# Expert-weight loads on ScalarE's queue in the last attention unit, rebalanced one-hots and a later rank sum, in a cross-attention and expert-mixture kernel

## What is computed

```python
def _L0_xattn_ref(q, k, v):            # 8 rows of one sequence are one head
    qh = q.reshape(b * h, d // h, m); kh = k.reshape(b * h, d // h, -1); vh = v.reshape(b * h, c // h, -1)
    qk = jnp.einsum('bdm,bdn->bmn', qh, kh) * scale
    sm = jax.nn.softmax(qk, axis=-1)
    return jnp.einsum('bmn,bcn->bcm', sm, vh).reshape(b, c, m)

def _L0_ffn_ref(x, gate_kernel, w0_kernel, w1_kernel, wo_kernel):   # 8 experts, top 2
    top_k_weights, top_k_indices = jax.lax.top_k(jnp.einsum('bsd,de->bse', x, gate_kernel), 2)
    top_k_weights = jax.nn.softmax(top_k_weights, axis=-1)
    combine = jnp.einsum('bsk,bske->bse', top_k_weights, jax.nn.one_hot(top_k_indices, 8))
    inter = jax.nn.silu(einsum(x, w0_kernel)) * einsum(x, w1_kernel)
    return jnp.einsum('bse,bsem,emd->bsd', combine, inter, wo_kernel)

x = x + _L0_xattn_ref(_layernorm(x), ctx_2048, ctx_2048)
x = x + _L0_ffn_ref(_layernorm(x), gate, w0, w1, wo)
```

## Time and profile before

| | us |
|---|---|
| median of 3 runs | 489.21 |
| lowest, highest | 484.64, 489.81 |
| the profiled execution | 489.81 |
| its span in the trace | 488.1 |

### The profile page before, as it was taken

One profiled execution on the slowest core, in us unless ns is written; L12 is line 12 of the kernel. 1 busy time (PEld: TensorE's weight loads), 2 busy tenths in 40 slices (PEclk: granted clock), 3 DMA queues, 4 the chain that ended last, 5 costly groups with the idle time before them and its releaser, 6 DMA issues.

```text
span 488.1 us, 10784 instructions
## 1 busy us (share of the span) xinstructions
PE 426.1 (87%) x3468; PEld 212.4 (44%) x3469; DVE 303.1 (62%) x636; ACT 267.1 (55%) x529; POOL 219.9 (45%) x244
## 2 busy tenths in 40 slices
PE   4857999889899999998666799999999999999991
PEld 4322343324343444333232455555555555566650
DVE  7799898898888888976867734343434343222220
ACT  2555898778778788977414444444444444222220
POOL 9544322181809052339628233454545454536231
PEclk9775899989889999999867999999999999999997
DMA  8757569685859682426994112333333333323322
GB/s 246 215 165 201 153 165 215 205 245 173 247 165 245 178 255 75 151 71 234 395 389 150 36 34 45 42 57 43 54 47 50 49 50 53 55 45 46 41 22 23
DMA packets 42246, 65.03 MB, mean 133 GB/s; under 512 B 6297, under 2 KB 32218, under 8 KB 42202
## 3 DMA queue, kind: packets, MB, share of 16 engines
q1 hardware_dynamic: 28570, 38.49, 28.0%
q0 software_dynamic: 11328, 23.86, 20.9%
q10 hardware_dynamic: 2304, 2.10, 1.4%
HBM read 39.53 MB, written 24.58 MB: 131 GB/s over the span
## 4 chain that ended last, share of the span: by engine, by line
PE 67%; DVE 10%; ACT 7%; DMA 6%; POOL 4%; issue 2%; ACTq 1%; SPq 1%; DVEq 0%; POOLq 0%
PE max_ps L1658 19%; PE pv_ps L1525 9%; PE pv_ps L1680 6%; PE ring_ps L1508 6%; ACT pt L851 5%; PE max_ps L1652 4%; PE max_ps L1384 4%; PE ring_ps L1680 4%; DVE mx L1026 4%; PE ring_ps L1616 3%; PE ring_ps L1405 2%; PE ring_ps L1675 2%; DMA Q<-mrow 2%; DMA Q<-q_img 2%; PE ring_ps L1416 2%
## 5 line engine op out<-in xcount | busy, mean ns | idle before, releaser
L1026 DVE TENSOR_REDUCE mx<-max_ps 128x4 f32<-128x1024 f32 x128 | 150.7, 1218 | 20.7 <-PE max_ps L1384 20.6
L851 ACT ACTIVATE pt<-ring_ps 128x512 f32<-128x512 f32 x256 | 139.2, 599 | 32.6 <-PE ring_ps L1508 29.1
L1658 PE MATMUL max_ps<-w_sb,pt 128*128 x224 | 101.6, 596 | 1.0 <-issue 1.0
L778 POOL DMA_INDIRECT out<-rb,sidx x34 | 54.8, 1613 | 81.3 <-DVE rb L1358 37.0
L1525 PE MATMUL pv_ps<-pt,w_sb 128*27 128x256 f32 (+2 forms) x1024 | 82.7, 408 | 0.7 <-ACT pvs L861 0.4
L1330 DVE TENSOR_TENSOR pt<-pt,max_ps 128x512 f32<-128x512 f32 x34 | 23.4, 688 | 68.4 <-issue 49.2
L1384 PE MATMUL max_ps<-K,Q 48*128 48x256 bf16 x512 | 54.5, 294 | 12.2 <-DVE mx L1026 12.0
L1508 PE MATMUL ring_ps<-Q,K 50*128 50x256 f16 x512 | 53.4, 289 | 11.5 <-ACT pt L851 9.2
L1658 PEld LDWEIGHTS max_ps<-w_sb,pt 128*128 128x128 f32 x224 | 40.3, 190 | 42.2 <-issue 42.0
L935 ACT ACTIVATE pt<-ring_ps 128x512 f32<-128x512 f32 x34 | 20.3, 598 | 68.1 <-PE ring_ps L1616 68.1
L1508 PEld LDWEIGHTS ring_ps<-Q,K 50*128 50x128 bf16 x512 | 15.1, 96 | 65.3 <-ACT pt L851 58.2
(11 more groups left out here) (230 smaller groups left out, 650.6 us busy)
## 6 DMA issues: line engine op xcount, KB each, us to landing
w_sb<-in_L_ffn_w_kernel POOLq DMA_DIRECT2D x16, 512.0 KB, 12.4
K<-k_img SPq DMA_DIRECT2D x14, 448.0 KB, 6.2
Q<-q_img SPq DMA_DIRECT2D x14, 448.0 KB, 7.6
k_img<-kpart SPq DMA_DIRECT2D x28, 192.0 KB, 3.8
q_img<-qpart SPq DMA_DIRECT2D x28, 192.0 KB, 3.4
wo_sb<-in_L_ffn_wo_kernel POOLq DMA_DIRECT2D x8, 512.0 KB, 14.4
acc<-pvs SPq DMA_DIRECT2D x6, 512.0 KB, 3.1
wo_sb<-in_ctx ACTq DMA_DIRECT2D x16, 128.0 KB, 3.9
```

The lines of the kernel that those rows point to most:

```text
L778: g.indirect_dma_start(xacc, bass.IndirectOffsetOnAxis(ap=sidx[sl.par][:, 0:1], axis=0), y_sb[sl.par], None, compute_op=ALU.add).then_inc( ...
L851: a.activation(pt[:, (2 * i + h) % PTN, :, :], bank(key)[:, :, :], ACT.Exp, scale=SCALE).then_inc(ring_read, 1)
L1026: v.tensor_reduce(mx[:, t % 2, :, :, p].rearrange("q mt h -> q h mt"), max_ps[n % 2][:, :, :, :], axis=AX.X, op=ALU.max).then_inc(max_read, 1)
L1658: last = nc.tensor.matmul(flat(max_ps[sl.par][:, bank_of]), lhsT=xT[sl.par][:, k * P:(k + 1) * P], rhs=weight(w, e, KC, k), start=(k == 0) ...
```

## The change

1. The 24 weight loads go from GpSimd to ScalarE. In tile 15 they stand behind each pair's exponentials and copies: w0(p) and wo(p) in each pair p, and w1(p - 2) too from pair 2. w1 of experts 6 and 7 come behind the last copy of the attention's output. GpSimd keeps the three powers.
2. In tile 15 the transposes and logits of units ST-3 and ST-2 stand one pair later, `unpermute(2)` one pair earlier, rank 0 in pair 6 (from pair 2). Rank 1 goes from pair 7 behind the transposes and logits of tile 14, with two wide matmuls into pv_ps behind it. VectorE's sum of rank 0 moves behind the norm of tile 14, that of rank 1 behind the norm of tile 15.
3. The one-hots are shared 17 (VectorE), 9 (ScalarE) and 6 (GpSimd), before 16, 8 and 8.
4. The spares are turned on TensorE ahead of the first transposes of slot 0 and reduced by VectorE ahead of the four products of line 1271. They are spread in slot 0 (TensorE) and read there by VectorE. Before this was in slots 0 and 1.

```diff
-    rows_at[T - 1, 1] = ST - 3
-    logits_at[T - 1, 2] = ST - 3
-    rows_at[T - 1, 3] = ST - 2
-    logits_at[T - 1, 4] = ST - 2
-    unperm_at = {(T - 2, 1): 0, (T - 2, 4): 1, (T - 1, 2): 2}
+    rows_at[T - 1, 2] = ST - 3
+    logits_at[T - 1, 3] = ST - 3
+    rows_at[T - 1, 4] = ST - 2
+    logits_at[T - 1, 5] = ST - 2
+    unperm_at = {(T - 2, 1): 0, (T - 2, 4): 1, (T - 1, 1): 2}
-    ranks_at = {(T - 1, 2): 0, (T - 1, 7): 1}
+    ranks_at = {(T - 1, 6): 0}
...
-        by_act = [(k, t) for k in range(TOPK) for t in range(2, T, 4)]
-        by_pool = [(k, t) for k in range(TOPK) for t in range(3, T, 4)]
+        by_act = [(0, t) for t in (3, 7, 11, 14)] + [(1, t) for t in (2, 5, 8, 11, 14)]
+        by_pool = [(0, t) for t in (5, 10, 15)] + [(1, t) for t in (4, 9, 13)]
+        by_dve = [(k, t) for k in range(TOPK) for t in range(T) if (k, t) not in by_act + by_pool]
...
@@ gpsimd @@
-            rows_landed(T - 1)
-            load_each(load_w0, range(E))
             rsqrt_last(0, 2, 1)
-            load_each(load_wo, range(4, E))
-            load_each(load_w1, range(3))
             rsqrt_last(2, 3, 2)
-            load_each(load_w1, range(3, E - 1))
-            load_each(load_wo, range(2))
             rsqrt_last(3, 4, 3)
-            load_w1(E - 1)
-            load_each(load_wo, range(2, 4))
...
@@ scalar, end of each pair's pass @@
+                if t == T - 1:
+                    if p == 0:
+                        a.wait_ge(mrow_in[1], T // 2 * 32)
+                    load_w0(p)
+                    load_wo(p)
+                    if p >= 2:
+                        load_w1(p - 2)
             evac_pv(T - 1)
+            load_w1(E - 2)
+            load_w1(E - 1)
...
@@ vector @@
             norm_last(normed_last[0:2], x2_last[0:2], 0, 1)
-            ranks(0)
...
             norm_last(normed_last[2:3], x2_last[2:3], 2, 2)
-            ranks(1)
+            ranks(0)
...
             norm_last(normed_last[3:4], x2_last[3:4], 3, 3)
+            ranks(1)
             choose(ST, unit_tiles[ST])
...
+            v.wait_ge(spare_turned, 1)
+            then(v.tensor_reduce(spare_any[:, :], y_ps[1][0:NT, 0, P // 2:P].bitcast(f16), axis=AX.X, op=ALU.max))
+            v.tensor_tensor(spare_diag[:, :], identh[0:NT, 0:NT], spare_any[:, 0:1].broadcast_to([NT, NT]),
+                            ALU.mult).then_inc(diag_done, 1)
             v.wait_ge(rows_picked, TOPK)
...
@@ tensor @@
             for m in range(ST - 1, UNITS):
                 turn_rows(m)
                 logits(m)
+                if m < UNITS - 1:
+                    rank(1)
+                    keep_warm(2, pv_ps)
...
             pe.wait_ge(slots_done, 1)
+            turn_spares()
             turn_x(Slots(0, 0))
...
                 if sl.peeled and sl.t == 0:
-                    turn_spares()
+                    spread_spares()
                 if sl.peeled and sl.t == 1:
-                    spread_spares()
                     slot_weights()
```

More of the change, by code:

```diff
@@ L649, in rsqrt @@
                 g.tensor_tensor(rstd[:, a:b], veps[:, a:b], mhalf[:, a:b], ALU.pow).then_inc(rstd_done, 1)
[L651 to L673, removed]
             g.wait_ge(consts, 2)
@@ L809, in _, with load_w0, load_w1, load_wo @@
         def _(a):
+            def load_w0(e):
+                a.dma_start(w0_sb[:, KC * e:KC * e + KC, :], w0_view[:, KC * e:KC * e + KC, :]).then_inc(w_in, 16)
+            def load_w1(e):
+                a.wait_ge(pv_full, 8 * (2 * e + 2))
+                a.dma_start(w1_sb[:, KC * e:KC * e + KC, :], w1_view[:, KC * e:KC * e + KC, :]).then_inc(w_in, 16)
+            def load_wo(e):
+                if e < E // 2:
+                    a.wait_ge(k_split, ST)
+                    for m in range(ST):
+                        a.wait_ge(ring_read, slots["v", m] + 1)
+                a.dma_start(wo_sb[:, FC * e:FC * e + FC, :], wo_view[:, FC * e:FC * e + FC, :]).then_inc(w_in, 16)
+            def load_each(load, experts):
+                for e in experts:
+                    load(e)
             def evac_v(g):
@@ L1232, in _ @@
                                 iota_t[:, None, :].broadcast_to([P, T, NTL]), ALU.is_equal).then_inc(rows_picked, 1)
-                onehots(k, [t for t in range(T) if (k, t) not in by_act and (k, t) not in by_pool])
+                onehots(k, [t for n, t in by_dve if n == k])
             v.wait_ge(told_full, 1)
@@ L1302, in stage, with spread_back @@
                     v.tensor_copy(wo_st[n][:, 0:FC // 2, :], wo_sb[:, bass.ds(e * FC, FC // 2), :]).then_inc(wo_copied[0], 1)
-            def turned_spares():
-                v.wait_ge(spare_turned, 1)
-                then(v.tensor_reduce(spare_any[:, :], y_ps[1][0:NT, 0, P // 2:P].bitcast(f16), axis=AX.X, op=ALU.max))
-                v.tensor_tensor(spare_diag[:, :], identh[0:NT, 0:NT], spare_any[:, 0:1].broadcast_to([NT, NT]),
-                                ALU.mult).then_inc(diag_done, 1)
-                then(v.tensor_scalar(rtok[:, :], tok[:, :], 1.0, None, ALU.max))
-                then(v.reciprocal(rtok[:, :], rtok[:, :]))
-            def slot_rows():
+            def spread_back():
                 v.wait_ge(spare_full, 1)
@@ L1316, in slot_rows @@
                 v.wait_ge(spare_read, 1)
+                then(v.tensor_scalar(rtok[:, :], tok[:, :], 1.0, None, ALU.max))
+                then(v.reciprocal(rtok[:, :], rtok[:, :]))
+            def slot_rows():
                 then(v.tensor_tensor(spare_of[:, :], spare_of[:, :], spare_own[:, :], ALU.add))
@@ L1337, in experts @@
                 if sl.peeled and sl.t == 0:
-                    turned_spares()
+                    spread_back()
                 if sl.peeled and sl.t == 1:
@@ L1475, in rank, with keep_warm @@
                 last.then_inc(ranks_full, 1)
-            def keep_warm(n):
+            def keep_warm(n, to=max_ps[1][:, 1]):
                 for _ in range(n):
-                    nc.tensor.matmul(flat(max_ps[1][:, 1]), lhsT=ident[:, :], rhs=flat(xn), start=True, stop=True)
+                    nc.tensor.matmul(flat(to), lhsT=ident[:, :], rhs=flat(xn), start=True, stop=True)
             def logits(m):
@@ L1584, in _ @@
                     else:
-                        pe.wait_ge(told_done, k * T // 2 + t // 4 * 2 + t % 4 + 1)
+                        pe.wait_ge(told_done, by_dve.index((k, t)) + 1)
                     last = nc.tensor.matmul(pv_ps[:, 0, 0:NTL], lhsT=onehot_s[:, k, t, :], rhs=onehot_t[:, k, t, :],
```

## The result

The changed kernel takes 497.93 us (median of 4 runs, 492.06 to 503.24), the kernel before 486.92 us in the same series. The ratio is 1.019, with a 95% interval of 1.0127 to 1.0252: slower, by about 9 us, where 487.0 was forecast and the range ended at 494.

The account below looks back on a forecast made before the run. The prediction took the chain of waits between attention and expert loop to bound the change's effect. Its terms, 1.3 - 0.4 - 1.9 - 1.3 = -2.3 us, gave 487.0 us from a median of 489.21, with an 8-in-10 range of 482.5 to 494.

Parts of the forecast that it names:

- What bounds the kernel now: Between attention and expert loop, a chain of waits through several engines decides; past 283 us gains or losses reach the end unchanged.
- Term 1: Weight loads moved to ScalarE, last attention unit: at 0.47 us an issue plus 0.04 between, tile 15's copy starts 1.3 us later.
- The walk's 1.3 us: Stepping through the last unit's new order with old start-to-start times: the copy of the last tile starts 1.3 us later.
- the first rival: ScalarE's DMA queue fills, each further issue lasting one load's drain, 1.39 us; slower, decisive from about three and a half loads down; chance 0.22.
- The walk's own bounds: Last tile's copy: 2.8 us later at 0.62 an issue, 5.2 later at GpSimd's 0.74, 1.6 earlier with issues free.
- Term 2: Ranks and warm matmuls before the last transposes: the two matmuls delay nothing; a better clock gives -0.4 us, ends 0 and -0.65.
- the prediction's own sign of being wrong in this term: At the last transposes, behind the ranks and warm matmuls: the clock still at half.
- The rival on the clock: Clock falls in the thinner last unit: last 16 attention matmuls and reordering, each 1.0 us, double; +2, total 489; chance 0.08.
- Term 3: One-hots shared 17, 9 and 6: their end moves from 263.23 to about 261.4, -1.9 us, bounds -1.6 and -2.0.
- Term 4: Spares at slots 0 and 1: TensorE's wait before the weight sums goes, -1.3 us, ends -1.4 and 0.
- The rest of the sum: The gains beside the moved loads: ranks and warm matmuls -0.4, one-hots -1.9, spares -1.3 us.

Follow-up runs that it names:

- the run with halves: The changed kernel with all weight loads issued by SyncE, each cut into two of half the rows (48 loads); one execution, 490.02 us.
- GpSimd's late loads: The changed kernel with only the eight w0 loads on ScalarE, the other 16 on GpSimd behind its last small power; 493.58 us, ratio 1.0117.

## Why the prediction was wrong, step by step

**What bounds the kernel now** held: the stretch between attention and expert loop decides, and E is 205.1 in both profiles. The weights landed in time, as forecast.

**Term 1, the failed step: "I take 0.47 plus 0.04 between two"** for all 22 issues. Eight of the first nine cost less than that (0.37 to 0.45). From the tenth on they cost what a load takes to drain, 1.47 us. The walk's 1.3 us became 11.9. The mechanism was there as the first rival, with chance 0.22, and its main piece of evidence against was misread: ten loads of x had gone out "in 0.60 each with the engines 0.99 busy", and there "some five were under way". Each of those was 0.13 MB in 128 rows, so five of them are a quarter of the bytes and two fifths of the rows that the expert loads had under way. The Trainium skill, quoted beside it (Perfetto Trace Analysis, DMA Instruction — HWDGE), says that such an instruction ends only when all its descriptors are made, and that these can be more than the buffer for them holds. The runs agree: a held issue took 0.94 to 2.62 us. The trace has one packet of data for each row, which fits a buffer that counts rows; that a row is one descriptor no run shows.

Two rows of the trace before, which the prediction did not use, bear on this price. SyncE's timeline:

```profile
94.26 0.39 SPq L494 DMA_DIRECT2D acc<-pvs  x1
94.76 1.67 SPq L463 DMA_DIRECT2D K<-k_img  x1
```

The first moves 0.5 MB in 128 rows of 4 KB and costs 0.39 us: an unheld issue of whole rows is cheaper than the 0.47 taken. The second costs 1.67 with under 300 rows under way. So a single long issue is not yet a full queue, and what held this one, or the seventh on SyncE (1.19), is not known; a full queue shows in that issue after issue is held.

**The size of that rival** was off too. "It decides from about three and a half loads down", with seven allowed the copy was to be 3.7 us late and with three 9.3: some 5.3 were under way and the delay was 11.9. The walk priced the drain at 1.39 us, where one issue in 1.47 was measured; it left the clock at 2.4 GHz, where scores, products and the last 16 matmuls fell to 1.2; and in the first 5.7 us the new queue landed only 1.1 MB. How the remainder splits between these was not tried. The walk's own bounds do not fit each other either: for 0.62 an issue, fifteen issues of 0.15 us more on top of the 1.3 make 3.5 us of delay, not 2.8; nothing else hangs on it.

**Term 2: "two take at most 2.7", so nothing.** The 2.7 came from five that took 6.79 us, "mostly at half the clock". They were not: ten records at 0.94 us each would take 9.4, and at full clock 4.9. Behind an attention that ends at full clock this is right: the four records take 1.96 us and TensorE waits 1.45 for VectorE behind them. The clock gain forecast there came too: the last transposes and logits took 0.41 and 0.58 us, not 0.66 and 0.99. In the changed kernel the warm matmuls took 3.76 us at half the clock and cost 1.5, and the last logits still took 0.99, the prediction's own sign of being wrong in this term. The rival on the clock had doubled the reordering, but not these.

**Term 3, one-hots: -1.9.** GpSimd's six took 6.58 us (6.1 forecast) and ScalarE's eighteen operations for nine 6.2 (6.4). From GpSimd's first one-hot to the end of the told matmuls it was 6.9 us instead of 8.4: -1.5, just outside the bound of -1.6.

**Term 4, spares: -1.3.** D is 11.9 instead of 13.5, -1.6, a little past the end of -1.4, and the wait of the earlier trace rows is gone. C, in front, is 0.6 longer (0.2 with the loads on GpSimd), of which the turned spares ahead of the transposes were to cost 0.1.

**The rest of the sum** would have stood: with the loads left on GpSimd it was -2.9 us (bounds -1.1 and -4.7), against -3.6 for terms 2 to 4. The third rival, the low clock, came on top of the first as its consequence, not instead of it: with the loads back on GpSimd and all else as changed the last 16 matmuls took 1.05 us, in the changed kernel 1.89.

## What to carry to other kernels

Before DMA issues are moved to an engine that also computes, count what they put under way: issued minus drained, in rows, at the pace of the new order. As long as that stays below what the queue holds, most issues cost some 0.4 us and hide; beyond it every issue costs one load's drain, and everything behind it in that stream waits. Such loads belong where little waits behind them, and even there look at what does: on SyncE it was the last rows' stores (up to 2.8 us in the run with halves), behind GpSimd's late loads the first gather (5.3 us). An old trace shows an issue's cost only for the fill that it had.

## What the runs showed of the hardware

- The hardware queues of ScalarE and SyncE each took about 1,500 to 1,900 rows (5.8 loads of 256 rows of 2 KB, 3.1 to 3.6 loads of 512 rows of 1 KB) before the issuer was held.
- An unheld issue of a 512-row load took 0.37 us, less than the 0.60 and 0.62 of the smaller loads of x and ctx in the earlier trace rows, and one of 128 rows of 4 KB 0.39; so neither rows nor bytes alone set this price.
- Behind the same wait of TensorE, 1.75 us, the 16 matmuls of the moved reordering ran at 1.2 GHz in six profiles (1.93 us) and at 2.4 GHz in three (1.07, the changed kernel's among these). What decides between the two levels there stays open.
